# Three stages of a four-layer network: the rotary step spread over three engines, the entry to the second stage taken lane by lane, and one round more in the first layer

## The reference

```python
x = L0_attn_inputs                                   # 4 x 512 x 128, taken as 2048 tokens
x = x + ln(attn0(ln(x)));  x = x + ln(ffn0(ln(x)))   # ffn0: silu(x @ gate) * (x @ up) @ down, 128 -> 384 -> 128
x = x + ln(attn1(ln(x)))                             # four pre-norm blocks: local + linear attention, gelu MLP
x = x + ln(ffn1(ln(x)))                              # soft mixture of experts: logits = x @ phi, softmax over batch and over slots
x = x + ln(attn2(ln(x)));  x = x + ln(ffn2(ln(x)))   # 16 heads of 8, causal; gelu MLP
x = x + ln(attn3(ln(x)))                             # scan block, MLP, then attention with 16 query and 4 key heads
x = x + ln(ffn3(ln(x)))                              # 8 experts, top-k
```

```python
def rms_norm(x):
    eps = jnp.asarray(jnp.finfo(x.dtype).eps, x.dtype)
    return x * jax.lax.rsqrt(jnp.mean(jnp.square(x), axis=-1, keepdims=True) + eps)
def apply_rope(x, cos, sin):
    half = x.shape[-1] // 2
    x1, x2 = (x[..., :half], x[..., half:])
    return jnp.concatenate([x1 * cos + x2 * sin, -x1 * sin + x2 * cos], axis=-1)
q = apply_rope(rms_norm(q), cos, sin) * q_gain
k = jnp.repeat(apply_rope(rms_norm(k), cos, sin), G, axis=1)
```

## Time and profile before

| | us |
|---|---|
| median of 3 runs | 3525.11 (3517.16 to 3526.27) |
| profiled execution, its own time | 3510.2 |
| its span, first to last instruction | 3508.2 |
| TensorE busy, share | 2871.1, 82% |
| VectorE busy, share | 2264.1, 65% |
| ScalarE busy, share | 1847.5, 53% |
| GpSimd busy, share | 474.3, 14% |
| mean granted TensorE clock | 0.899 of full |

### The profile page before, as it was taken

One profiled execution on the slowest core, in us unless ns is written; L12 is line 12 of the kernel. 1 busy time (PEld: TensorE's weight loads), 2 busy tenths in 40 slices (PEclk: granted clock), 3 DMA queues, 4 the chain that ended last, 5 costly groups with the idle time before them and its releaser, 6 DMA issues.

```text
span 3508.2 us, 75846 instructions
## 1 busy us (share of the span) xinstructions
PE 2871.1 (82%) x31896; PEld 2297.6 (65%) x31896; DVE 2264.1 (65%) x5990; ACT 1847.5 (53%) x4106; POOL 474.3 (14%) x535
## 2 busy tenths in 40 slices
PE   5788887788888668888885879997888899786895
PEld 3566665466666457777774667876767688575474
DVE  4766656665666489888887755457575634764527
ACT  3566665456666468777774444344544433454232
POOL 1110101210000132222221101120010211002000
PEclk8899998889999789988997899997999999797897
DMA  2000000000000100000001000010010000101000
GB/s 93 1 2 1 1 2 1 1 1 1 2 1 1 52 7 7 7 7 7 7 1 43 20 3 25 1 49 2 3 49 3 25 1 14 37 3 49 1 1 25
DMA packets 16997, 48.95 MB, mean 14 GB/s; under 512 B 1168, under 2 KB 9616, under 8 KB 14096
## 3 DMA queue, kind: packets, MB, share of 16 engines
q1 hardware_dynamic: 16656, 44.10, 3.6%
HBM read 41.99 MB, written 2.10 MB: 13 GB/s over the span
## 4 chain that ended last, share of the span: by engine, by line
PE 53%; DVE 32%; ACT 10%; issue 3%; POOL 1%; DMA 0%; DVEq 0%; SPq 0%; POOLq 0%; ACTq 0%
PE ps L324 7%; DVE LN L2009 5%; PE ps L315 5%; PE ps L1887 3%; PE ps L1349 3%; PE ps L381 3%; PE ps L468 3%; DVE M L484 2%; PE ps L289 2%; DVE LN L2022 2%; PE ps L1360 2%; DVE RS L239 2%; ACT LN L263 2%; PE ps L1831 2%; ACT LN L297 1%
## 5 line engine op out<-in xcount | busy, mean ns | idle before, releaser
L297 ACT COPY LN<-ps 128x512 f32<-128x512 f32 (+4 forms) x560 | 287.2, 550 | 295.8 <-PE ps L289 63.0
L276 POOL TENSOR_TENSOR RS<-RS,MISC 128x4 f32<-128x4 f32 x184 | 188.8, 1026 | 1499.1 <-DVE RS L258 793.3
L484 DVE TENSOR_REDUCE M<-ps 128x6 f32<-128x768 f32 x256 | 241.5, 955 | 132.6 <-PE ps L468 93.8
L289 PE MATMUL ps<-cons,LN 128*128 128x128 f32 x672 | 127.4, 329 | 185.3 <-ACT LN L263 91.5
L289 PEld LDWEIGHTS ps<-cons,LN 128*128 128x128 f32 x672 | 90.9, 166 | 228.8 <-ACT LN L263 82.0
L2009 DVE TENSOR_TENSOR LN<-LN 128x1024 f32<-128x1024 f32 (+2 forms) x192 | 219.9, 1145 | 27.9 <-ACT LN L297 16.2
L381 PE MATMUL ps<-LN 32*128 32x256 f32 x1024 | 188.2, 441 | 54.5 <-DVE LN L520 31.6
L315 PE MATMUL ps<-LN,wAB 128*128 128x512 f32 x384 | 202.5, 660 | 15.5 <-DVE LN L952 15.5
L1887 PE MATMUL ps<-LN,wAB 128*128 128x128 f32 x1024 | 153.0, 313 | 73.8 <-ACT LN L297 73.3
L628 DVE TENSOR_REDUCE M<-ps 128x12 f32<-128x1536 f32 x64 | 112.4, 1757 | 150.4 <-PE ps L371 150.4
L384 PE MATMUL ps<-LN 32*128 32x256 f32 x1024 | 202.4, 474 | 4.3 <-DVE M L484 4.3
(11 more groups left out here) (361 smaller groups left out, 7395.0 us busy)
## 6 DMA issues: line engine op xcount, KB each, us to landing
LN<-frame SPq DMA_DIRECT2D x16, 1024.0 KB, 4.9
wAB<-wb SPq DMA_DIRECT2D x16, 256.0 KB, 2.7
LN<-frame SPq DMA_DIRECT2D x8, 512.0 KB, 3.5
LN<-wd SPq DMA_DIRECT2D x8, 512.0 KB, 6.4
wAB<-wa SPq DMA_DIRECT2D x1, 3840.0 KB, 16.4
wCs<-wc SPq DMA_DIRECT2D x1, 2336.0 KB, 10.6
XA<-xin SPq DMA_DIRECT2D x8, 256.0 KB, 7.9
y<-XA SPq DMA_DIRECT2D x8, 256.0 KB, 2.3
```

The source lines that it names most:

```text
L276: pool.e.tensor_tensor(c.r[:, 40:44], c.r[:, 36:40], mhalf, ALU.pow).then_inc(*c.G.inc((k, "rstd")))
L289: ins = pe.e.transpose(ps[:, n * 128:(n + 1) * 128], src[:, n, :], ident)
L297: act.e.copy(dst, ps).then_inc(*c.A.inc(named(k, done)))
L484: return dve.e.tensor_reduce(cols[:, 2 - 2 * h:4 - 2 * h, :, q.at], src, X_AX, ALU.max, negate=True)
```

## The change

It has three parts, and moves some loads.

1. *The rotary step.* The squares go from VectorE to ScalarE, behind the scaled copies. The factor 0.125 and the epsilon go into ScalarE's root, with a constant column `epsc` that VectorE fills at the start. The keys' four copies go to GpSimd; TensorE waits for them ahead of the keys' transposition.
2. *The entry lane by lane.* The barrier between stage one and the entry goes. Lane 0 takes groups 0 to 4 as soon as its own work in stage one ends, lanes 1 to 3 groups 5 to 7. `phi` and the first four weight blocks are loaded before stage one ends, as soon as lane 3 no longer reads the weights that lie there.
3. *One round more in layer 0.* In "l0f" ScalarE normalizes in one round; TensorE's transposition and ScalarE's copy come in the next, and all that follows one round later.

```diff
@@ pe_l0
             k = (g, "l0f")
             yield
+            yield
             pe.wait_ge(c.A, (k, "normed", 3))
             pe_tr4(pe, c, k, XN, 0, c.A)
@@ pe_mid
             pe.wait_ge(c.D, (k, "roped"))
             pe_tr4(pe, c, k, v["QK"][:, :, 0:128], 0, c.D, "qa")
+            pe.wait_ge(c.G, (k, "repeated"))
             pe_tr4(pe, c, k, v["KR"], 1, c.A, "ka")
@@ dve_mid
-            dve.wait_ge(c.A, (k, 1, "qkv"))
-            dve.e.tensor_tensor(sq, QK, QK, ALU.mult).then_inc(*c.D.inc())
-            dve.wait_ge(c.D)
-            dve.e.tensor_reduce(rb, sq.rearrange("p t (h d) -> p (t h) d", d=8), X_AX, ALU.add).then_inc(*c.D.inc())
-            dve.wait_ge(c.D)
-            dve.e.tensor_scalar(rb, rb, 0.125, EPS, ALU.mult, ALU.add).then_inc(*c.D.inc((k, "ms")))
+            dve.wait_ge(c.A, (k, "qk_sq"))
+            dve.e.tensor_reduce(rb, sq.rearrange("p t (h d) -> p (t h) d", d=8), X_AX, ALU.add).then_inc(*c.D.inc((k, "ms")))
...
-            dve.e.tensor_tensor(QK, sq, un, ALU.add).then_inc(*c.D.inc())
-            dve.wait_ge(c.D)
-            for t in range(4):
...
-                ins = dve.e.tensor_copy(kr4, k3_.unsqueeze(2).to_broadcast([128, 4, 4, 8]))
-            ins.then_inc(*c.D.inc((k, "roped")))
+            dve.e.tensor_tensor(QK, sq, un, ALU.add).then_inc(*c.D.inc((k, "roped")))
@@ act_mid
+            act.wait_ge(c.A, (k, 1, "qkv"))
+            act.e.activation(v["sq"], QK, ACT.Square).then_inc(*c.A.inc((k, "qk_sq")))
             yield
             act.wait_ge(c.D, (k, "ms"))
-            act.e.activation(v["rb"], v["rb"], ACT.Sqrt).then_inc(*c.A.inc((k, "rms")))
+            act.e.activation(v["rb"], v["rb"], ACT.Sqrt, scale=0.125, bias=epsc).then_inc(*c.A.inc((k, "rms")))
@@ pool_mid
-            yield from idle(5)
+            yield from idle(3)
+            pool.wait_ge(c.D, (k, "roped"))
+            for t in range(4):
...
+                ins = pool.e.tensor_copy(kr4, k3_.unsqueeze(2).to_broadcast([128, 4, 4, 8]))
+            ins.then_inc(*c.G.inc((k, "repeated")))
+            yield from idle(2)
@@ new
+        def pe_entry(pe, c, groups):
+            for g in groups:
+                k = ("in2", g)
+                yield
+                yield
+                pe.wait_ge(c.A, (k, "normed", 3))
+                pe_tr4(pe, c, k, ZX[:, 4 * g:4 * g + 4, :], 0, c.A)
+
+        def act_entry(act, c, groups):
+            for g in groups:
+                k = ("in2", g)
+                yield
+                act.wait_ge(DD[0], ((4, "l1p"), "x"))
+                act_norm(act, c, k, XG[g], ZX[:, 4 * g:4 * g + 4, :])
+                yield
+                act_copy(act, c, k, XTA[:, 512 * g:512 * g + 512], c.ps[0][:, :], "tr", "xT")
...
@@ phase1
+                yield from entry(eng, c, (0, 1, 2, 3, 4) if c.n == 0 else (4 + c.n,))
@@ pe_program
-            phase1(pe, lanes1(banks), pe_l0, pe_l1)
+            phase1(pe, lanes1(banks), pe_l0, pe_l1, pe_entry)
             ended(PD, "p1")
             sync_all(pe, "p1")
-            banks = Banks()
-            run_in(pe_in, pe, "in2", ZX, XTA, lanes(banks))
-            ended(PD, "p2in")
-            sync_all(pe, "p2in")
...
@@ sp_program
-            sync_all(sp, "p1")
+            sp.wait_ge(PD[3], ((("l1", 1, 1), 3), "k_pe"))
             e.dma_start(phi, wb[:, 0:2048]).then_inc(got_phi, 16)
+            sp.wait_ge(PD[3], ((7, 2, "mlp"), "sum"))
             for q in range(4):
                 load_w(q)
+            sync_all(sp, "p1")
             e.dma_start(wCs[:, :], wc).then_inc(got_wc, 16)
```

39 lines of the change are left out of this document (22 added, 17 removed).

## The result

| | before | after |
|---|---|---|
| median of the runs, first measurement | 3521.14 | 3476.8 |
| ratio of the runs (95% interval) | | 0.989 (0.9867 to 0.9913) |
| the same kernel measured once more | 3514.05 | 3478.93, ratio 0.9897 (0.9879 to 0.9915) |
| profiled execution: own time, span | 3510.2, 3508.2 | 3473.26, 3471.4 |
| mean granted TensorE clock | 0.899 | 0.905 |

By the ratios of the two measurements the change makes the kernel 36 to 39 us faster, where 26.7 were forecast. The predicted 3498 was too high by 21. The range went down to 3476, and 3476.8 lies 0.8 us inside it.

A forecast was written before the change was run, and what follows sets the result against it. No engine is full, so waits at each changed place count. Terms -16.3 + 3.7 - 9.7 - 4.4 = -26.7 take the profiled 3510.2 us to 3483; with the median 15 above, 3498 us, range 3476 to 3518.

The forecast's parts named there:

- A: Entry to stage two: only lane 3's group stays behind the last addition, 7.5 us in place of 23.8, -16.3.
- B: Last 13 rounds of stage one: seven entry groups move there, three pieces find no gap, +3.7, bounds 0 and +45.
- C: Layer 0's extra round: half of the transposition waits won, less two rounds' idle time, -9.7, bounds -24.6 and +13.4.
- D: Rotary step in both halves: shorter VectorE period of 6.9 us, less GpSimd's copies, -4.4, bounds -6 and +8.7.
- Rival 4: Entry: stage two would wait for data, not the groups, so no entry gain; sum -10.4, 3515 us, chance 0.03.
- the bound of +45: Last rounds of stage one: seven entries each cost their whole 6.5 us chain across four engines.
- I take half of 24.6: Layer 0: of eight TensorE waits on ScalarE's normalization summing to 24.6 us, 12.3 us are won.
- All eight waits: Layer 0, four lanes in two halves: TensorE's transposition waits on ScalarE's normalization, 24.6 us in sum.
- rival 1: Layer 0: the extra round gains nothing, waits move to the next chain; 3508 us (chance 0.17) or 3522 (0.07).
- Rival 2: Rotary step: GpSimd's copies of 1.19 us become the tail, perhaps excluding VectorE; 3504 to 3511 us, chance 0.12.
- Rival 3: Last rounds of stage one: entries stall all engines, 6.5 us each, sum +15, 3540 us, slower; chance 0.04.
- D's end: Rotary step: the favourable bound of -6, where TensorE's 0.35 us wait for the rotated queries' transposition does not come.

The follow-up runs named there:

- the round behind the copy: Kernel before, with one round more in layer 0's second norm behind transposition and copy instead of between normalization and transposition: 3522.33 us, ratio 1.0018.
- the late normalization: Kernel before, with the extra layer 0 round but ScalarE's normalization one round later too, together with transposition and copy: 3526.16 us, ratio 1.0029.
- the sixth: Kernel after, with one round more also between normalization and transposition of layer 0's first norm: 3479.59 us, ratio 0.9899.

## Why the prediction was right or wrong

| term | predicted | trace, before against after | timed runs |
|---|---|---|---|
| A, the entry behind the barrier | -16.3 | -16.9, and -1.6 in stage two with the clock | |
| B, seven groups in the last rounds | +3.7 | +4.0 | A and B together -9.8 alone |
| C, the round | -9.7 | -16.9 (7.8 and 9.1) | -13.7 alone, -17.6 in the kernel after |
| D, the rotary step | -4.4 | -7.3 | -3.9 (-8 to +1) |
| sum | -26.7 | -38.7 | -36 to -39 |

**A** held. The chain that is left, one group and the barrier, was put at 7.5 and is 6.9. What the prediction missed is the loads: it took them for work that was hidden anyway. Phi was hidden by the 23.8 us that the change removes. Left in its place it would have cost 5.0. Rival 4 was right to look at phi, but on the wrong side: not that the entry would save nothing, but that phi would have been next.

**B** held in sum and not in its pieces. Lane 0's first statistics did delay L952, by 1.4, but this was given back by 1128; what stays comes from lane 0's groups between 1136 and 1152 and from lane 2's statistics (1.3), and no cost of the transposition between the up-projections shows: with it, both pairs take from 1160.02 to 1165.84, less than the one piece of 6.34 had the earlier trace rows, as the second pair ran at the higher clock (1.88 us, the first 3.67). With a clock of 0.84 the same order costs 8.4. So the bound of +45 was far off, that the sum was met so closely is luck in part, and the term's real uncertainty was the clock.

**C** is the term furthest from its forecast, -16.9 for -9.7. The step of the sum that was mis-sized is "I take half of 24.6": it counted removed waits, with the clock as it was. All eight waits on the normalization are gone in the kernel after, but TensorE's idle time in layer 0 fell by far less than 24.6 us. In the first half it is 36.2 on the average of the seven kernels and 39.2 of the four without the round; in the second it is 48.2 before and 49.8 after, and 49.7 in the kernel without the round. What got shorter is the time that the same matmuls take: 4.8 us in the first half by these averages, 10.7 in the second from before to after, where the clock was 0.90 instead of 0.86.

This count doesn't part the two causes cleanly, as a faster TensorE can also just wait longer. But where the same order ran twice, the second half's layer 0 with the round alone and in the kernel after, 4.4 us less of busy time made it 4.3 shorter, at the same idle time (49.65 and 49.75). So a good part of the gain came as clock, for which the prediction had no term, and part of the waits came up again elsewhere, as rival 1 had it. How much each is isn't shown.

One of the new waits can be named. It is that of lane 0's transposition in the second half, after:

```profile
604.88 0.63 PE L289 MATMUL ps<-cons,LN 128*128 128x128 f32 x4 [3.10 <-ACT LN L334]
```

The normalization had ended 8 us before. TensorE waits here for a PSUM bank, since lanes 0 and 2 have the same two, and lane 2's gelus (L334), which free it, stand behind lane 1's exponentials and a table load of 1.28 us. This is the table load that the prediction put at nothing; there are 22 in this stretch instead of 21.

That the round in this place makes layer 0 shorter is shown: the second half takes 197.8 to 202.1 us in the seven kernels with it, 206.9 in the four without, 209.5 with the round behind the copy and 213.7 with the late normalization. The late normalization shows too that ScalarE's order has to change with TensorE's. Why this order gets the higher clock isn't shown. Where the waits are of another norm (the first), 15.6 us of them gave 4.4. Waits are thus no price by themselves.

**D** has two mistakes of the same sign. The period was right (6.9 predicted, 6.94), as was the square's estimate (0.74 for 0.7). GpSimd's copy takes 0.29 us and not 0.454, and above all the four were added to the last lane's path as 1.8, though TensorE transposes the queries first, from 2358.51 on, while the copies run from 2358.52 to 2359.52. They are nearly hidden: the keys' weight load waits 0.35 us for them, and the eight transpositions take 2.18 us instead of the 1.97 that they took before. The cover was in the code's order and was not read from it.

**The rivals.** Rival 1 (the round gains nothing) is out in its result by the round alone; its mechanism, waits that move, is part of what the traces show. Rival 2 (the copies become the tail) is out at their real size. At the size that it assumed, it costs 10.8 by the trace (5.4 a half) and 7.7 by the runs, within the 6.0 to 13.1 that it gave itself over the forecast, but by TensorE's order and not by the shared port. Rival 3 (the entries stall the last rounds) is out.

**The level.** Of the 21 us by which 3498 was too high, 10 are the sum's. The other 11 come from the step to the median: it was put 15 above the profiled execution as before, and was 3.5 above. The lower end of the range was said to hold all eight waits (14.9 beyond C), D's end (1.6) and part of B; with all of B (3.7) these give 3477.8 and not 3476. So it is luck that 3476.8 lies inside.

**What stays open.** How much of C is waits and how much clock. Why TensorE's clock comes out higher in layer 0's second half with the round, and at 0.94 in the last rounds in five kernels with entry and round and at 0.84 in the sixth and in those without the round. In the kernel after one low stretch begins at 1156.6, in the 4.75 us that TensorE idles ahead of 1160.02, but the one at 2484.4 begins in none, and no run here set the clock by itself. Nor is it shown what makes up all of the 9 to 11 us between the sum of the parts and the whole, nor that it is more than noise; 4.5 of them are this last stretch.

## What to carry to other kernels

Where a step waits in order for another engine and foreign work stands behind it, give its producer a round's lead and let the foreign work go between, and do it on both engines' orders; moving only one of them made this kernel slower. Then look at the idle time of the waiting engine, and not at the wait that is gone: here part of it came up again elsewhere. When a stretch that hid loads is shortened, move the loads with it and count them as the next thing late. Before a step is priced as added to a path, look at what the waiting engine does first; and don't read a difference of one clock step (here 4 us) out of a single profiled execution.

## What was not expected of the hardware

Layer 1 took 369.6 to 370.0 us or 373.7 to 373.8 in 27 of the 28 halves of these 14 profiles, at a mean granted clock of 0.93 or 0.91; its instructions are the same in all. The Trainium skill (TensorE: Matmul & The Clock Gate, "Part 1") calls the number of matmuls at the low clock run-variable; the traces agree. The timed runs of the kernel before, 3508 to 3529 us, go with the clock too: the run of 3508.6 had a mean of 0.899, that of 3528.6 one of 0.892.

GpSimd's copy of 128x128 with repeated source took 0.29 us against VectorE's 0.16 (4 in 0.63), while its power step on 128x4 took 1.59.
